# Perceiver block, cross-attention: maxima from row tiles in four visits per group, units in pairs, one stacked key buffer

## The chip, the cores and the metric

One NeuronCore of a Trainium2 chip runs the whole program. The metric is device time in microseconds, the median of several executions; lower is better. The engines are PE (matmuls), DVE (VectorE), ACT (ScalarE), POOL (GpSimd) and SP (SyncE, which here issues DMAs).

## The reference

A block of three layers on x (8 batches of 128 rows, 512 wide). Only the first layer is changed:

```python
x = x + xattn(layernorm(x), ctx_1024, Wq, Wk, Wv, Wo)      # the layer of this change
x = x + attn(layernorm(x), ...)                            # quantised self-attention
x = x + ffn(layernorm(x), router_w, w1, w2)                # eight experts, top two

# xattn: T_q = 128, T_c = 2048, 16 heads of 32
Q = (query @ Wq.T).reshape(B, T_q, 16, 32)
K = (context @ Wk.T).reshape(B, T_c, 16, 32)
V = (context @ Wv.T).reshape(B, T_c, 16, 32)
attn = softmax(einsum('bqhd,bkhd->bhqk', Q, K) / sqrt(32))
out = einsum('bhqk,bkhd->bqhd', attn, V).reshape(B, T_q, 512) @ Wo.T
```

## The kernel before

Cross-attention works batch by batch (b = 0 to 7), and in a batch by groups of four heads (g = 0 to 3). The batches 1 to 6 are a hardware loop on every engine (`Fori(1, B - 1)`); batches 0 and 7 are written out. Operands of a product are split into float16 high and low parts, and a product is three terms (`mm_terms`).

**Projections.** K of a group is made in four blocks of 512 columns (`project_k`), V of eight heads in eight pieces of 2 x 256 columns (`project_v`). All go through two PSUM banks, proj0 and proj1, in the order of the list `USES`; one use of a bank is 12 matmuls of 512 columns or 24 of 256. ACT empties a bank (`copy_v`, or `split_k`, which writes k_hi), DVE makes k_lo, and `wait_bank` lets PE write it again. Some V pieces are cut into thirds and laid between score units (`FILL`, `fill_after`).

**Stacked keys.** For the scores, k_hi, k_lo, k_hi of a head are stacked on 96 partitions of ks, by 12 DMAs that SP issues (`stack_k`, L265); ks has two buffers, so that a group is stacked while the one before is still read. A 97th row (L299, set to 1) meets the negative maximum in qs.

**A group.** First the maxima: eight units u, each two matmuls of 96 x 512 into one of two two-bank tiles sc (`scores_for_max`, L734), and one DVE maximum over 1024 columns (`maximum`, L537). PE lays one third of the next group's K between two units. Then DVE turns the maxima into a diagonal (L545), PE into a row (L749), ACT writes it to qs (L402). Then, for eight units: transposed scores (`scores_transposed`, L763, eight matmuls), the exponential on ACT (L416), and probabilities times V (`times_v`, L780, f32, four column tiles, recorded as 16 matmuls). PE runs one unit of scores ahead of the values.

**Denominators.** DVE sums five of the eight probability units into acc_v (L556, L559), POOL the other three into acc_g (L333, L338), and PE multiplies both, in halves, by ones (`denominators`, L791: 16 f32 matmuls, 32 records).

**Around it.** SP loads the context of the next batch in eight slots' worth of 0.5 MB through two stage buffers (`load_ctx`, L249); ACT writes the high part (L379), DVE the low part (L511), and DVE also the high part of two of the eight. x is loaded in one DMA, and DVE makes its statistics (L578) before group 0. The projection of the output (L821) of batch b - 1 stands in batch b, before group 0. The weights of self-attention are loaded and quantised by POOL beside this.

The experts' loop (`Fori(1, E_ - 1)`, and SP's `Fori(1, E_)`) is the other hardware loop that the change touches.

Of the kernel before, what the change touches and what calls it, by code (L numbers as in the profile page):

```python
# [64 lines left out]
def cross_attention(nc, x, ctxT, wqT, wkT, wvT, woT, wiT, qoT, weights_q, wmax, wscale, x1, x1_stats, ident, ident16, ones, ones16):  # L65

    with ExitStack() as c:
# [3 lines left out]
        def sem(name):  # L73
            return c.enter_context(nc.semaphore(name))

        stage = sb("stage", [P, 2, 2, 512], f32)
# [8 lines left out]
        ks = sb("ks", [P, 2, GH, S], f16)  # L85
# [9 lines left out]
        mx = sb("mx", [P, GH, 2], f32)  # L95
# [19 lines left out]
        sc = [c.enter_context(nc.psum_tensor(f"sc{i}", [P, 1024], f32)) for i in range(2)]  # L115
# [3 lines left out]
        x_in = sem("x_in")  # L119
# [4 lines left out]
        stage_in = [sem(f"stage_in{i}") for i in range(2)]  # L124
# [17 lines left out]
        ks_in = [sem(f"ks_in{i}") for i in range(2)]  # L142
# [8 lines left out]
        stage_hi_v = sem("stage_hi_v")  # L151
# [16 lines left out]
        W_ORDER = (2, 1, 0)  # L168
        w_stage = [probs[:, 0:2, :], probs[:, 2:4, :], v_sb[:, 1, 0:8, :]]
# [5 lines left out]
        USES = ([("k", 0, i) for i in range(KB)] + [("v", 1, i) for i in (0, 1, 2)]  # L175
                + [("k", 1, i) for i in range(KB)] + [("v", 1, 3)]
                + [("k", 2, i) for i in range(KB)] + [("v", 1, i) for i in (4, 5)]
                + [("k", 3, i) for i in range(KB)] + [("v", 1, i) for i in (6, 7)] + [("v", 0, i) for i in range(8)])

        FILL = {0: [(1, i) for i in (6, 7)], 1: [(1, i) for i in range(8, 12)],  # L180
                2: [(1, i) for i in range(12, 16)], 3: [(0, i) for i in range(10, 16)]}
# [11 lines left out]

        def use_k(b, g, kb):
            return 8 + 32 * b + USES.index(("k", g, kb))

        def use_v(b, half, n):
            at = USES.index(("v", half, n))
            return 8 + 32 * b + at if half else 32 * b + at - 24

        def bank(use_in_body):
            return use_in_body % 2

        DVE_HIGH = (2, 3)

        def high_parts_done(b, s):

            if first_batch(b):
                return stage_hi, s + 1
            if s in DVE_HIGH:  # L210
                return stage_hi_v, 2 * (b - 1) + DVE_HIGH.index(s) + 1
            return stage_hi, 8 + 6 * (b - 1) + (s if s > 3 else s + 2) - 1
# [4 lines left out]
        def fill_after(g, unit, last):  # L217

            pieces = FILL[g] if not (last and g == 3) else []
            thirds = [(half, piece, term) for half, piece in pieces for term in range(3)]  # L220
            if unit < 0:
                return thirds[0:3]
            rest = thirds[3:]
            return rest[unit * len(rest) // UNITS:(unit + 1) * len(rest) // UNITS] if unit < UNITS else []

        def wait_k_stacked(eng, b, g):

            if isinstance(b, int) and b == 0 and g == 0:
                return
            n = 2 * b + (g - 1) // 2 + 1 if g else 2 * b  # L230
            eng.wait_ge(ks_in[(g - 1) % 2], 192 * n)

        with nc.Block() as block:

            @block.sync
            def _(sp):
# [4 lines left out]
                def load_ctx(b, s):  # L241
                    n = 8 * b + s
                    if not isinstance(b, int):
                        sp.compute_val(b * (D * S) * 4)
                    if not (first_batch(b) and s < 2):

                        wait_each(sp, (stage_lo, n - 1))
                    src = ctx_v[bass.ds(b, 1), :, 2 * (s % 2):2 * (s % 2) + 2, 512 * (s // 2):512 * (s // 2) + 512]
                    sp.dma_start(stage[:, s % 2], src.rearrange("a p c s -> (a p) c s")).then_inc(stage_in[s % 2], 16)  # L249
# [7 lines left out]
                def stack_k(b, g):  # L257

                    waits = [(proj_act, use_k(b, g, KB - 1) + 1), (k_low, 16 * b + 4 * g + KB)]
                    if g >= 2 or not first_batch(b):  # L260
                        waits.append((s_ready, 8 * (4 * b + g - 1)))
                    wait_each(sp, *waits)
                    for row, part in ((0, k_hi), (HD, k_lo), (2 * HD, k_hi)):
                        for j in range(GH):
                            sp.dma_start(ks[row:row + HD, g % 2, j, :], part[HD * j:HD * j + HD, :]).then_inc(ks_in[g % 2], 16)  # L265
# [4 lines left out]
                load_w(1)  # L270
                load_ctx(0, 2)
                for s in range(3, 8):
                    load_ctx(0, s)
                sp.dma_start(x1[:, :, :], x.rearrange("b p d -> p b d")).then_inc(x_in, 16)
                load_w(2)
                sp.dma_start(wo[:, :, :], woT.rearrange("(c p) d -> p c d", p=P)).then_inc(wo_in, 16)

                def body(b, last):
                    if not first_batch(b):
                        stack_q(b)  # L280
                    stack_k(b, 0)
                    stack_k(b, 1)
                    if not last:
                        load_ctx(b + 1, 0)
                        load_ctx(b + 1, 1)
                    stack_k(b, 2)
                    stack_k(b, 3)
                    if not last:
                        for s in range(2, 8):
                            load_ctx(b + 1, s)  # L290

                body(0, False)
                with sp.Fori(1, B - 1) as b:
                    body(b, False)
# [3 lines left out]
            def _(gp):  # L298
                gp.memset(ks[QK:P, :, :, :], 1.0).then_inc(rows_set, 1)  # L299
# [23 lines left out]
                def body(b, last):  # L323
                    for g in range(G):
# [4 lines left out]

                        gp.wait_ge(e_ready, e + 4)  # L330
# [5 lines left out]
                        gp.wait_ge(e_ready, e + 7)  # L336
                        gp.wait_ge(sum_g, 8 * b + 2 * g + 1)
# [1738 lines left out]
```

## Time and profile before

| what | us |
|---|---|
| median of 3 executions | 2024.96 (2024.83 to 2025.88) |
| the profiled execution | 2023.88 |
| its span, first to last instruction | 2022.4 |
| PE busy | 1767.7 (87%) |
| DVE busy | 1206.1 (60%) |
| ACT busy | 777.4 (38%) |
| POOL busy | 338.0 (17%) |
| mean granted clock of TensorE | 0.941 of full |

Busy time is the union of the instructions of an engine. A matmul's recorded duration overlaps that of the next, since they are pipelined; the distance between starts is its price. Waits are put down to what released them.

### The profile page before, as it was taken

What the parts mean: (1) busy time and instruction counts of PE and PEld (TensorE: products, weight loads), DVE (VectorE), ACT (ScalarE), POOL (GpSimd) and SP (SyncE); (2) the same over time, 40 slices, a digit from 0 to 9 for tenths busy, and PEclk for the clock granted to TensorE, in tenths of its full rate; (3) what the DMA queues carried; (4) which work ended last, traced back from release to release, by engine and by line L of the source; (5) the groups of instructions that cost most, each with busy time, mean ns of one, the idle gap of its engine ahead of it and who ended that gap; (6) DMA issues with size and microseconds to landing.
All of it is one profiled execution on the core that took longest, in us unless ns stands there. A gap on an engine that the chain in (4) does not pass through costs nothing. (4 is left out here: it accounts for less than half of the span.)

```text
span 2022.4 us, 43611 instructions
## 1 busy us (share of the span) xinstructions
PE 1767.7 (87%) x18170; PEld 1171.1 (58%) x18170; DVE 1206.1 (60%) x1469; ACT 777.4 (38%) x955; POOL 338.0 (17%) x308
## 2 busy tenths in 40 slices
PE   6899999999999999999999999774527999999991
PEld 4547557556556556656656655553314777777771
DVE  4477576467467367367377377485765665566632
ACT  4334244244244244344334333228434444444420
POOL 3122111010010010011011046240140000000003
PEclk9999999999999999999999999785857999999996
DMA  6334323133133133133123234400056544554404
GB/s 218 71 89 121 82 66 95 41 85 95 41 85 95 41 84 95 41 79 99 42 72 97 51 87 118 142 1 2 2 188 233 181 164 158 178 192 171 151 14 138
DMA packets 101310, 202.43 MB, mean 100 GB/s; under 512 B 24876, under 2 KB 24876, under 8 KB 101022
## 3 DMA queue, kind: packets, MB, share of 16 engines
q1 hardware_dynamic: 91438, 170.74, 28.8%
q0 software_dynamic: 9712, 29.23, 4.5%
q8 instruction: 140, 2.29, 0.5%
q14 instruction: 20, 0.16, 0.0%
HBM read 127.57 MB, written 18.91 MB: 72 GB/s over the span
## 5 line engine op out<-in xcount | busy, mean ns | idle before, releaser
L537 DVE TENSOR_REDUCE mx<-sc 128x1 f32<-128x1024 f32 x256 | 303.1, 1215 | 23.4 <-PE sc L734 23.2
L416 ACT ACTIVATE probs<-sc 128x1024 f32<-128x1024 f32 x256 | 258.6, 1023 | 146.1 <-PE sc L763 144.1
L559 DVE TENSOR_TENSOR acc_v<-acc_v,probs 128x1024 f32<-128x1024 f32 x96 | 164.4, 1713 | 155.0 <-ACT probs L416 154.4
L396 ACT ACTIVATE k_hi<-proj 128x512 f16<-128x512 f32 x128 | 76.4, 597 | 445.5 <-PE proj L712 445.5
L333 POOL TENSOR_TENSOR acc_g<-probs 128x1024 f32<-128x1024 f32 x32 | 75.5, 2358 | 840.5 <-ACT probs L416 840.5
L734 PE MATMUL sc<-ks,qs 96*128 96x512 f16 x512 | 156.1, 387 | 36.5 <-DVE mx L537 32.1
L699 PE MATMUL proj<-w_hi,ctx_hi 128*128 128x256 f16 x1024 | 156.4, 275 | 20.1 <-DVE ctx_lo L511 20.1
L780 PE MATMUL po<-probs,v_sb 128*32 128x128 f32 x4096 | 163.3, 280 | 9.6 <-ACT probs L416 7.4
L947 DVE SCALAR_TENSOR_TENSOR w_lo<-stage_w,w_hi 128x2048 f16<-128x2048 f32 x64 | 144.4, 2289 | 43.5 <-ACT w_hi L941 43.3
L763 PE MATMUL sc<-qs,ks 97*128 97x128 f16 x2048 | 158.8, 222 | 0.7 <-ACT qs L402 0.7
L699 PE MATMUL proj<-w_hi,ctx_lo 128*128 128x256 f16 x1024 | 155.6, 275 | 0.0
L699 PE MATMUL proj<-w_lo,ctx_hi 128*128 128x256 f16 x1024 | 155.6, 275 | 0.0
L515 DVE SCALAR_TENSOR_TENSOR k_lo<-proj,k_hi 128x512 f16<-128x512 f32 x128 | 88.0, 689 | 113.1 <-ACT k_hi L396 112.7
L1952 PE MATMUL po<-h_lo,w_hi 128*128 128x321 f16 x512 | 154.1, 301 | 0.0
L1952 PE MATMUL po<-h_hi,w_lo 128*128 128x321 f16 x512 | 154.0, 301 | 0.0
L1952 PE MATMUL po<-h_hi,w_hi 128*128 128x321 f16 x512 | 154.0, 301 | 0.0
L712 PE MATMUL proj<-ctx_hi,w_hi 128*128 128x512 f16 x512 | 135.0, 386 | 16.2 <-issue 16.2
L763 PEld LDWEIGHTS sc<-qs,ks 97*128 97x128 f16 x2048 | 122.0, 99 | 38.4 <-issue 29.5
L1788 ACT ACTIVATE hf<-ph 128x321 f32<-128x321 f32 x128 | 56.2, 440 | 220.6 <-PE ph L1936 204.5
L712 PE MATMUL proj<-ctx_hi,w_lo 128*128 128x512 f16 x512 | 135.0, 387 | 0.0
L712 PE MATMUL proj<-ctx_lo,w_hi 128*128 128x512 f16 x512 | 134.6, 386 | 0.0
L780 PEld LDWEIGHTS po<-probs,v_sb 128*32 128x32 f32 x4096 | 98.0, 110 | 58.8 <-issue 37.1
(274 smaller groups left out, 2781.0 us busy)
## 6 DMA issues: line engine op xcount, KB each, us to landing
stage_w<-in_w SPq DMA_DIRECT2D x64, 1024.0 KB, 6.0
stage<-in_ctxT SPq DMA_DIRECT2D x64, 512.0 KB, 4.5
ks<-k_hi SPq DMA_DIRECT2D x256, 128.0 KB, 2.4
ks<-k_lo SPq DMA_DIRECT2D x128, 128.0 KB, 2.4
wq_f<-in_wiT POOLq DMA_DIRECT2D x24, 256.0 KB, 3.0
xbuf<-zeros SPq DMA_DIRECT2D x20, 256.0 KB
obuf<-o_sb POOLq DMA_DIRECT2D x16, 256.0 KB, 2.6
xg<-xbuf POOLq DMA_DIRECT2D x14, 256.0 KB, 5.6
```

The costliest lines, as they stand in the source:

```text
L396: act.activation(k_hi[:, 512 * kb:512 * kb + 512], proj[bank(USES.index(("k", g, kb)))][:, :], ACT.Copy, scale=1.0 / WSCALE).then_inc(proj ...
L416: act.activation(probs[:, u % 4, :], sc[u % 2][:, :], ACT.Exp, scale=1.0 / sqrt(HD)).then_inc(e_ready, 1)
L515: dve.scalar_tensor_tensor(k_lo[:, 512 * kb:512 * kb + 512], proj[bank(USES.index(("k", g, kb)))][:, :], 1.0 / WSCALE, k_hi[:, 512 * kb:51 ...
L537: dve.reduce_max(mx[:, u // 2, u % 2:u % 2 + 1], sc[u % 2][:, :], AX.X).then_inc(m_read, 1)
L559: dve.tensor_tensor(acc_v[:, :], acc_v[:, :], probs[:, (0, 0, 1, 3)[part], :], ALU.add).then_inc(sum_v, 1)
L699: last = pe.matmul(out, x_part[:, kb, e, at:at + P], w_part[:, 2, e, wv], start=term == 0 and e == 0, stop=term == 2 and e == EC - 1)
L712: last = pe.matmul(proj[bank(at)][:, :], w_part[:, 1, e, P * g:P * g + P], x_part[:, kb, e, :], start=term == 0 and e == 0, stop=term == 2 ...
L734: last = pe.matmul(sc[u % 2][:, 512 * i:512 * i + 512], qs[0:QK, 4 * g + j, :], ks[0:QK, g % 2, j, at:at + 512], start=True, stop=True)
L763: last = pe.matmul(sc[u % 2][:, 512 * i + P * j:512 * i + P * j + P], ks[0:QKM, g % 2, j, P * ck:P * ck + P], qs[0:QKM, 4 * g + j, :], sta ...
L780: last = pe.matmul(po[HD * j:HD * j + HD, 0:T], v_sb[:, g // 2, ck, at:at + HD], probs[:, u % 4, 512 * i + P * j:512 * i + P * j + P], sta ...
L947: dve.scalar_tensor_tensor(w_lo[:, s], stage[:, s % NST], WSCALE, w_hi[:, s], ALU.mult, ALU.subtract).then_inc(stage_lo, 1)
L1952: last = pe.matmul(po[i][:, 0:CAP], w_part[:, s, f, P * i:P * i + P], h_part[:, at, :], start=q == 0 and f == 0 and n == 0, stop=q == FQ - ...
```

## The change

1. **Maxima.** ks is no longer read for the maxima. A visit takes one block of 512 keys and all four heads: four matmuls of 32 rows (`tile_position=(32 j, 0)`), q_hi by k_hi, one head per bank of sc, which is now one four-bank tile. One DVE reduction covers the four banks. A group has four visits, and PE lays a whole use of a proj bank between two.
2. **One ks buffer.** ks has room for one group. `stack_k(b, g)` waits for all transposed scores of the group before, and transposed scores of the group wait for it.
3. **Order of uses.** `USES` has eight uses per group: five in the maximum phase (V, the last K block of this group, V, V, V), three in the score phase (K blocks 0 to 2 of the next group). Blocks and pieces of the next batch's first group are made in group 3.
4. **Pairs.** Transposed scores of two units, then values of the two units before, then two thirds of a use. A leading third stands before the first pair.
5. **Denominators.** DVE sums units 0, 1, 4, 5, 6; POOL 2, 3, 7, then adds acc_v, then folds 1024 columns to 512; PE has four f32 matmuls left.
6. **Loads.** Four stage buffers (`SLOTS`) in place of two; ACT makes all high parts of the context; x in two DMAs, the first for batch 0; statistics of the other batches and their roots in the groups 0 and 1 of batch 0. PE waits for wo before batch 0 in place of after it.
7. **Loops.** All loops touched are made by `nc.Fori(..., hint_back_edge=True)`, in cross-attention and in the experts.

```diff
-        ks = sb("ks", [P, 2, GH, S], f16)
+        ks = sb("ks", [P, GH, S], f16)
-        sc = [c.enter_context(nc.psum_tensor(f"sc{i}", [P, 1024], f32)) for i in range(2)]
+        sc = c.enter_context(nc.psum_tensor("sc", [P, GH, 512], f32))
+        FILL_A = [("v", 0, 4), ("k", 0, 3), ("v", 0, 5), ("v", 0, 6), ("v", 0, 7),
+                  ("v", 1, 0), ("k", 1, 3), ("v", 1, 1), ("v", 1, 2), ("v", 1, 3),
+                  ("v", 1, 4), ("k", 2, 3), ("v", 1, 5), ("v", 1, 6), ("v", 1, 7),
+                  ("v", NEXT_V, 0), ("k", 3, 3), ("v", NEXT_V, 1), ("v", NEXT_V, 2), ("v", NEXT_V, 3)]
+        USES = []
+        for g in range(G):
+            USES += FILL_A[5 * g:5 * g + 5] + [("k", g + 1, kb) for kb in range(KB - 1)]
...
                     waits = [(proj_act, use_k(b, g, KB - 1) + 1), (k_low, 16 * b + 4 * g + KB)]
-                    if g >= 2 or not first_batch(b):
-                        waits.append((s_ready, 8 * (4 * b + g - 1)))
+                    if g or not first_batch(b):
+                        waits.append((s_ready, 8 * (4 * b + g)))
...
-                with sp.Fori(1, B - 1) as b:
+                with nc.Fori(1, B - 1, engines=(mybir.EngineType.SP,), hint_back_edge=True) as b:
...
+                        gp.wait_ge(sum_v, at + 4)
+                        gp.wait_ge(sum_g, at + 2)
+                        gp.tensor_tensor(acc_g[:, :], acc_g[:, :], acc_v[:, :], ALU.add).then_inc(sum_g, 1)
+                        gp.wait_ge(sum_g, at + 3)
+                        gp.tensor_tensor(acc_g[:, 0:512], acc_g[:, 0:512], acc_g[:, 512:1024], ALU.add).then_inc(sum_g, 1)
...
+                def maximum(b, g, kb):
+                    dve.wait_ge(m_ready, 16 * b + 4 * g + kb + 1)
+                    dve.tensor_reduce(mx[:, :, kb], sc[:, :, :], AX.X, ALU.max).then_inc(m_read, 1)
...
+                def body(b, last, steps):
+                    for g in range(G):
+                        maximum(b, g, 0)
+                        maximum(b, g, 1)
+                        if g == 3 and not last:
+                            split_ctx(b + 1, 3)
+                        maximum(b, g, 2)
+                        split_k(b, g, 3)
+                        maximum(b, g, 3)
+                        maxima_to_diag(b, g, steps)
...
+                        for part in range(4):
+                            add_probs(b, g, part)
...
+                            if part and (g < 3 or not last):
+                                nb, ng = (b, g + 1) if g < 3 else (b + 1, 0)
+                                split_k(nb, ng, part - 1)
...
+                    for j in range(GH):
+                        rows = slice(HD * j, HD * j + HD)
+                        last = pe.matmul(sc[:, j, :], q_hi[rows, g, :], k_hi[rows, 512 * kb:512 * kb + 512],
+                                         start=True, stop=True, tile_position=(HD * j, 0))
                     last.then_inc(m_ready, 1)
...
+                        scores_for_max(b, g, 0)
+                        if ahead:
+                            project(b, 8 * g)
+                        scores_for_max(b, g, 1)
+                        project(b, 8 * g + 1)
+                        scores_for_max(b, g, 2)
+                        if ahead:
+                            project(b, 8 * g + 2)
+                        scores_for_max(b, g, 3)
+                        if ahead:
+                            project(b, 8 * g + 3)
+                        if g:
+                            denominators(b, g - 1)
+                        elif not first:
                             denominators(b - 1, 3)
+                        if ahead:
+                            project(b, 8 * g + 4, range(2))
+                        maxima_to_row(b, g)
+                        if ahead:
+                            project(b, 8 * g + 4, range(2, 3))
+                        for pair in range(4):
+                            if ahead and pair == 0:
+                                project(b, 8 * g + 5, range(LEAD))
+                            scores_transposed(b, g, 2 * pair)
+                            scores_transposed(b, g, 2 * pair + 1)
+                            if pair:
+                                times_v(b, g, 2 * pair - 2)
+                                times_v(b, g, 2 * pair - 1)
+                            if g == 0 and pair == 0 and not first:
+                                project_out(b - 1)
+                            for i in range(LEAD + 2 * pair, LEAD + 2 * pair + 2) if ahead else ():
+                                project(b, 8 * g + 5 + i // 3, range(i % 3, i % 3 + 1))
```

## Rows read from the trace of the kernel before

**Rows 1.** Timeline of PE: start us, duration, line, operation, count, idle before
```profile
74.05 0.60 PE L734 MATMUL sc<-ks,qs 96*128 96x512 f16 x2 [4.23 <-DMA ks<-k_hi]
...
227.84 3.60 PE L821 MATMUL misc<-wo_sb,ot 128*128 128x512 f32 x8
...
1007.44 3.60 PE L821 MATMUL misc<-wo_sb,ot 128*128 128x512 f32 x8
...
1286.74 5.42 PE L821 MATMUL misc<-wo_sb,ot 128*128 128x512 f32 x8 [1.41 <-DVE ot L568]
```

**Rows 2.** Timeline of PE inside two batches, around and between score phases
```profile
671.30 1.08 PE L780 MATMUL po<-probs,v_sb 128*32 128x128 f32 x32
...
714.34 0.61 PE L699 MATMUL proj<-w_hi,ctx_hi 128*128 128x256 f16 x4
714.78 0.60 PE L699 MATMUL proj<-w_hi,ctx_lo 128*128 128x256 f16 x4
...
717.54 0.64 PE L780 MATMUL po<-probs,v_sb 128*32 128x128 f32 x16 [0.82 <-ACT probs L416]
718.11 0.62 PE L763 MATMUL sc<-qs,ks 97*128 97x128 f16 x8
718.57 0.60 PE L699 MATMUL proj<-w_hi,ctx_hi 128*128 128x256 f16 x4
719.10 0.64 PE L780 MATMUL po<-probs,v_sb 128*32 128x128 f32 x16
...
733.41 0.64 PE L791 MATMUL po<-acc_v,ones 128*32 128x128 f32 x16
...
734.43 0.61 PE L734 MATMUL sc<-ks,qs 96*128 96x512 f16 x2
...
735.73 0.60 PE L734 MATMUL sc<-ks,qs 96*128 96x512 f16 x2
```

**Rows 3.** Groups by line, whole span: busy us, mean ns of one, idle before
```profile
L537 DVE TENSOR_REDUCE mx<-sc 128x1 f32<-128x1024 f32 x256 | 303.1, 1215 | 23.4 <-PE sc L734 23.2
L416 ACT ACTIVATE probs<-sc 128x1024 f32<-128x1024 f32 x256 | 258.6, 1023 | 146.1 <-PE sc L763 144.1
...
L734 PE MATMUL sc<-ks,qs 96*128 96x512 f16 x512 | 156.1, 387 | 36.5 <-DVE mx L537 32.1 <-DMA ks<-k_hi 4.2
...
L515 DVE SCALAR_TENSOR_TENSOR k_lo<-proj,k_hi 128x512 f16<-128x512 f32 x128 | 88.0, 689 | 113.1 <-ACT k_hi L396 112.7
...
L333 POOL TENSOR_TENSOR acc_g<-probs 128x1024 f32<-128x1024 f32 x32 | 75.5, 2358 | 840.5 <-ACT probs L416 840.5
...
L578 DVE BATCH_NORM_STATS2 st<-x 128x6 f32<-128x512 f32 x8 | 4.8, 679 | 3.1 <-DMA x<-in_x 3.1
```

**Rows 4.** Timeline of PE in self-attention: row tiles of 32 and of 17 rows
```profile
1358.75 0.62 PE L1359 MATMUL pa<-k_int,q_int 32*128 32x128 f16 x16 [3.78 <-ACT q_int L1127]
1359.13 0.66 PE L1345 MATMUL pb<-mask_r,mask_l 17*128 17x512 bf16 x4
```

**Rows 5.** Timeline of PE behind a back edge of cross-attention's loop
```profile
675.42 1.51 PE L712 MATMUL proj<-ctx_hi,w_hi 128*128 128x512 f16 x4 [3.04 <-issue]
676.72 1.91 PE L712 MATMUL proj<-ctx_hi,w_lo 128*128 128x512 f16 x4
```

**Rows 6.** Windows, the experts: PE, PEld, DVE, ACT, POOL busy, clock, DMA share, GB/s
```profile
1550.00:1980.00 430.00, 428.64 (x3153) 308.96 (x3151) 248.71 (x362) 173.48 (x227) 21.99 (x39) 1.00 0.43 150
```

**Rows 7.** SP's issues in the timeline, and the landing of the stacked keys (L265)
```profile
31.30 4.21 SPq L276 DMA_DIRECT2D wo_sb<-in_woT  x1
...
63.40 2.77 SPq L265 DMA_DIRECT2D ks<-k_hi  x4
...
745.02 2.42 SPq L265 DMA_DIRECT2D ks<-k_hi  x4
...
DMA to landing us min/median/max: 2.2/2.4/5.4
```

**Rows 8.** The page's DMA issues: count, KB each, us to landing
```profile
wo_sb<-in_woT SPq DMA_DIRECT2D x1, 1024.0 KB, 16.7
```

More of the change, by code:

```diff
@@ L141, in cross_attention @@
         k_low = sem("k_low")
[L142 removed]
+        ks_in = sem("ks_in")
         m_ready = sem("m_ready")
@@ L192, in stacked_q, with use @@
                     for row, part in ((0, q_hi), (HD, q_hi), (2 * HD, q_lo)) for j in range(GH)]
-        def use_k(b, g, kb):
-            return 8 + 32 * b + USES.index(("k", g, kb))
-        def use_v(b, half, n):
[L198 to L212, printed above, removed]
+        def use(b, at):
+            n = FIRST_USES + 32 * b + at
+            if isinstance(b, int) and b == -1 and at == LAST_V:
+                return 0
+            if isinstance(b, int) and b == B - 1 and at > LAST_V:
+                return n - 1
+            return n
@@ L214, in first_batch, with unit_scores @@
+        def unit_scores(u):
+            return sc[:, 2 * (u % 2):2 * (u % 2) + 2, :].rearrange("p a n -> p (a n)")
         def first_batch(b):
             return isinstance(b, int) and b == 0
[L217 to L224, printed above, removed]
@@ L226, in wait_k_stacked @@
         def wait_k_stacked(eng, b, g):
[L228 to L231, printed above, removed]
+            if not (isinstance(b, int) and b == 0 and g == 0):
+                eng.wait_ge(ks_in, 192 * (4 * b + g))
         with nc.Block() as block:
@@ L671, in wait_bank @@
                 def wait_bank(b, at):
[L673 to L680 removed]
+                    if isinstance(b, int) and b == -1 and at in (LAST_V, LAST_V + 3):
+                        return
@@ L694, in project_v @@
-                    kb, at = piece // 4, P * (piece % 4)
-                    wv = slice(256 * half, 256 * half + 256)
-                    for term in terms:
-                        x_part, w_part = mm_terms(ctx_hi, ctx_lo, w_hi, w_lo)[term]
-                        for e in range(EC):
-                            last = pe.matmul(out, x_part[:, kb, e, at:at + P], w_part[:, 2, e, wv],
-                                             start=term == 0 and e == 0, stop=term == 2 and e == EC - 1)
-                    if c == 1 and 2 in terms:
+                    out = proj[at % 2][:, 256 * c:256 * c + 256]
@@ new lines, in project_v @@
+                    kb, col = piece // 4, P * (piece % 4)
+                    if c == 0 and term == 0:
+                        wait_bank(b, at)
+                        if half == NEXT_V:
+                            pe.wait_ge(stage_lo, 8 * (b + 1) + 2 * kb + 2)
+                    wv = slice(256 * (half % 2), 256 * (half % 2) + 256)
+                    x_part, w_part = mm_terms(ctx_hi, ctx_lo, w_hi, w_lo)[term]
+                    for e in range(EC):
+                        last = pe.matmul(out, x_part[:, kb, e, col:col + P], w_part[:, 2, e, wv],
+                                         start=term == 0 and e == 0, stop=term == 2 and e == EC - 1)
@@ L1886, in _ @@
                 body(0, False)
-                with dve.Fori(1, E_ - 1) as e:
+                with nc.Fori(1, E_ - 1, engines=(mybir.EngineType.DVE,), hint_back_edge=True) as e:
                     body(e, False)
```

509 lines of the change are left out of this document (251 added, 258 removed).

## The prediction, made before the result was known

> **What bounds the kernel now.** I read the timeline of PE first, at its landmarks [rows 1]. The output projection of cross-attention (L821) starts at 227.84 and five batches later at 1007.44, so a batch takes 155.9 us; the first maximum scores start at 74.05 and the last output projection ends at 1292.2, so the change has 1292 of 2022 us to work on. Then the timeline inside a batch [rows 2]: PE rows follow each other without a gap through most of a group, so PE sets the pace of this stage. The same rows give its prices. Four V matmuls of 256 columns take 0.44 us (714.34 to 714.78), so one use of a proj bank, 24 of these or 12 K matmuls of twice the width, takes 2.62. Six matmuls of 512 columns take 1.30 (734.43 to 735.73), 0.217 each. Transposed scores of a unit take 0.46 (718.11 to 718.57). The V matmuls before a values unit take 0.53 in place of 0.44 (718.57 to 719.10), and a single values unit 0.57 (717.54 to 718.11), while two in a row take about 0.92 until the last one drains (671.30): 0.46 each, 0.09 to go in and 0.12 to come out. Denominators take 1.02 (733.41 to 734.43). The groups by line add what is idle [rows 3]: PE waits 32.1 us in all for the maxima (L537), 4.0 per batch; the wait for the first exponential of a batch is 0.82 (717.54). DVE's maximum of 1024 columns takes 1.215, ACT's exponential 1.02, k_lo 0.69, GpSimd's add 2.36. None of them is a rival of PE today in their sums (DVE is busy for 60% of the span), so an edit pays in full only where it shortens PE's own list.
>
> **What PE loses.** Sixteen maximum matmuls of a group are 3.5 us. After, there are four visits of four row-tiled matmuls with 32 rows each, on q_hi and k_hi without the stacked copies. The trace has such tiles in self-attention [rows 4]: sixteen of 128 columns start within 0.38 us, 0.024 each, and four of 512 columns are over in 0.66. So four in a visit run side by side: 0.22, and with the 0.21 of changes into and out of a tile mode less their overlap I take 0.38. That is 1.5 per group, a gain of 2.0 (bounds: 0.22 and 0.87 per visit). Denominators fall from 32 recorded matmuls to 8: 0.76. Units in pairs save four of eight changes around the values: 4 x 0.21 = 0.8. Sum per batch 4 x 3.56 = 14.2. The Trainium skill ("TensorEngine Tiling (Array Packing)", Key Properties) says that a change of tiling mode drains TensorE. The 0.09 and 0.12 agree; by that rule the four new visits put back what the pairs take away, and my 0.38 holds it.
>
> **The loops.** At the back edge of PE's loop there is a gap of 3.04 us put down to issue, and the clock falls for the next matmuls (four of them from 676.72 take 1.71 in place of 0.86) [rows 5]. The loop has six passes, so five such edges; I take 3.0 and 1.0 of clock per batch as removed. In the experts PE is busy for 428.6 of 430 us [rows 6], so the same edit there gives nothing. The Trainium skill ("Runtime: NRT & Kernel Launch", Instruction fetch mechanics) says that a taken branch outside the fetched pages stalls for a fetch; the trace agrees in the first loop and not in the second. With the 4.0 and 0.8 of waits gone, PE alone would need 155.9 - 14.2 - 4.0 - 4.8 = 132.9 per batch.
>
> **What is added, in order of time.** The stacked keys ks lose their second buffer. Until now the stack of a group was sent a whole phase early; now its last part, k block 3, is projected between the visits 1 and 2 of its own group, and transposed scores wait for the landing. Follow it from the start of visit 2. Scores end and DVE starts after 0.55; a maximum over four banks is 2 x 1.07 + 0.12 = 2.25 (from the 1.215); k_lo is queued behind it, 0.65; SP 0.1. SP then issues 12 DMAs, four in 2.42 us (745.02) with a pause of 0.05 behind, 0.62 each, and the median landing is 2.4 after its issue [rows 7]: 11 x 0.62 + 2.4 = 9.2, with the longer sets 9.3. With 0.05 the stack is there 12.9 after visit 2. PE has until then: visit and V use 3.0, again 3.0, denominators with their change 0.36, two thirds of a V use 1.75, the row 0.4, the last third 0.87 and the leading K third 0.87, in all 10.25. PE waits 2.65 in every group. Queued behind that wait are all later matmuls of the group, then ACT's exponentials and both engines that add. In group 3 the low part of a context slot stands between two maxima, 0.5 more.
>
> A second wait: with pairs, DVE makes k_lo of block 0 of the next group only after the sum that waits for exponential 4. From pair 2 on: scores 0.63, exponential 1.02, sum 1.25, k_lo 0.69 and links 0.1 are 3.7 to 4.1; PE comes to that bank after 0.92 + 1.13 + 0.87 = 2.94. I take 0.75 per group (bounds 0 and 1.2). The clock: a gap of 3.04 was followed by half speed for some three us; I expect that after half of the new gaps, 1.7 each, less what hides the second wait: 0.6 per group (bounds 0 and 1.7). GpSimd's two added folds (2.36 and about 1.2) end some 4 us after a group and the denominators come 12 after it: nothing on the path, hidden by four proj uses; uncovered they show only in the last group. DVE's maxima save 0.1 us per group, off the path. The visits must not outrun them: 2.25 + 0.55 + 0.06 = 2.86 against 3.0, so no wait, but only 0.14 to spare.
>
> Steady batch: 132.9 + 4 x (2.65 + 0.75 + 0.6) + 0.5 = 149.4.
>
> **The ends.** At the start seven uses stand before the first visit in place of fifteen, x is split in two loads, four slots let the context run ahead; but PE waits for wo, the last load, before its body. wo was issued by 35.5 (31.30 + 4.21) and landed 16.7 later, near 51 [rows 7, 8]; with the same bytes and fewer waits I put the first visit at 50 (bounds 45 and 58). Batch 0 carries seven statistics of x (0.6 each by the x8 row, 4.8 in all) ahead of the maxima of group 1, and sixteen weight maxima between the sums: 8 more. The last batch: three groups of 35.4, which is 16.25 + 2.65 to the scores, then 15.1 (0.92 of scores, 1.73 of K, three times 0.92 + 1.13 + 1.73, and 1.13 of values), 0.75 and 0.6; one output projection 3.5; group 3 without fill: 18.9 to the scores, eight exponentials 9.3, then GpSimd's chain 2.36 + 2.36 + 1.2 + links = 6.2, denominators, reciprocal and product 1.6, projection 5.4: 41.4. Sum 151. The end: 50 + 8 + 7 x 149.4 + 151 = 1254.8, against 1292.2: 37 us less. The rest of the program keeps its 730 us. The profiled execution took 2023.88, 1.1 under the median, its span 2022.4; taken from the median, 2024.96 - 37 = 1988.
>
> **The rivals.** *The stack is hidden*: landings follow faster or the visits are slower than DVE thinks, and the 2.65 and the clock go: 4 x 3.25 + 0.5 per batch, about 106 in all, 1880. For it: SP's rows are issue times, and PE may be slowed by something else ahead. Against: 12 issues of 0.62 stand in the sets that I read, and nothing sends them earlier. *The stack takes longer, and the change is slower*: the only stack for which PE waited took from 63.40 to 74.05, 10.65 in place of 9.3 [rows 1, 7]. 1.35 x 32 is 43: 2031. It decides from 37 / 32 = 1.2 us more per group. Against: that one ran beside the loads of the start. *Row tiles don't run side by side*, the change not doing what it says: 0.87 per visit, three of them ahead of the stack, 1.5 x 32 = 47: 2035; the tile rows speak against it. *The announced loops help the experts too*, by the fetch rule: five edges of 3, 1973; the window without a gap speaks against it.
>
> **How the numbers follow.** Forecast 0.55 (from no lost clock, 1969, and no second wait, 1945, to a start at 58 and a fall after each gap, about 2023); hidden stack 0.15; longer stack 0.20; serial tiles 0.05; experts' loops 0.05. Within 0.2% (4 us, about what this kernel's times can tell from no change) 0.06, out of the upper forecast and the smaller half of the longer stack. Faster 0.74, slower 0.20. The range 1930 to 2034 reaches into the hidden stack by part and over the longer one.
>
> **What would show it.** Right: PE's first transposed scores wait for the DMA of ks by 2 to 3 us in each group; visits 3.0 us apart with four bank-wide matmuls in under 0.4; a batch near 149; no issue gap at the back edge; a K matmul waiting for k_lo in pair 2; the first visit near 50. Wrong if the wait on ks is absent (time near 1880), if it passes 4 us, if GpSimd's reads stretch DVE's maxima, or if DVE falls behind PE's visits, since a late maximum delays visit and stack alike.

## The result, and the profile of the changed kernel

The changed kernel takes 2085.3 us (median of 4, 2079.67 to 2101.22) against 2024.89: 1.032 times as long [1.0293, 1.0347]. Forecast were 1988 and a range from 1930 to 2034. It is slower by 3.2%, and the loss lies in cross-attention: its last output projection ends at 1356.6, where 1292.2 was before and 1254.8 forecast. The program behind it keeps its time (2085.1 - 1356.6 = 728.5 against 730.2).

The first part of the profile's page, after; for each engine busy us, share of the span and instructions:

```profile
PE 1701.8 (82%) x17402; PEld 1138.9 (55%) x17402; DVE 1186.7 (57%) x1333; ACT 784.5 (38%) x972; POOL 450.3 (22%) x372
```

PE is busy for 66 us less and the span is 63 us longer, so PE is idle for about 129 us more. What it waits for stands in the table of PE's waits (us in total, times, longest):

```profile
PE sc L805 <- DMA ks<-k_hi: 87.3, 32, 7.1
PE sc L772 <- DVE mx L567: 69.5, 18, 8.2
...
PE proj L747 <- DVE k_lo L535: 21.7, 29, 1.2
...
PE po L830 <- POOL acc_g L348: 5.7, 1, 5.7
```

The first and third rows are the two waits of the forecast (2.65 x 32 and 0.75 x 29). The second was forecast as nothing, but for the 8 us that batch 0 was given; for maxima PE waited 32.1 before [rows 3]. The landmarks in PE's timeline that answer to [rows 1] are the output projections of batches 0, 1, 5 and 7:

```profile
251.24 3.65 PE L862 MATMUL misc<-wo_sb,ot 128*128 128x512 f32 x8
...
408.29 3.65 PE L862 MATMUL misc<-wo_sb,ot 128*128 128x512 f32 x8
...
1041.51 5.35 PE L862 MATMUL misc<-wo_sb,ot 128*128 128x512 f32 x8
...
1350.30 6.31 PE L862 MATMUL misc<-wo_sb,ot 128*128 128x512 f32 x8 [1.40 <-DVE ot L598]
```

Over the same five batches as in the prediction, a batch is (1041.51 - 251.24) / 5 = 158.1 long (155.9 before, 149.4 forecast); the shortest takes 157.1. The granted clock of 0 to 1290 was 0.98 before and is 0.95 (the two windows, columns as in [rows 6], before ahead of after):

```profile
0.00:1290.00 1290.00, 1200.09 (x12796) 759.76 (x12797) 775.42 (x802) 490.15 (x617) 233.22 (x168) 0.98 0.31 82
```

```profile
0.00:1290.00 1290.00, 1095.12 (x11563) 703.90 (x11563) 731.94 (x644) 478.97 (x613) 317.00 (x206) 0.95 0.30 80
```

Now the place at which PE waits for a maximum in a steady batch, the step from group 2 to group 3. The first visit of group 3 starts at 652.76, the second at 660.23. First PE's timeline (start, duration, line; in brackets the idle time ahead and what ended it), then DVE's and POOL's:

```profile
637.00 1.07 PE L805 MATMUL sc<-qs,ks 97*128 97x128 f16 x16 [2.13 <-DMA ks<-k_hi]
...
647.04 1.04 PE L747 MATMUL proj<-ctx_hi,w_hi 128*128 128x512 f16 x4 [0.63 <-DVE k_lo L535]
...
660.23 0.61 PE L772 MATMUL sc<-k_hi,q_hi 32*128 32x512 f16 x4 [4.34 <-DVE mx L567]
660.77 1.89 PE L747 MATMUL proj<-ctx_hi,w_hi 128*128 128x512 f16 x4
```

```profile
649.77 1.21 DVE L529 TENSOR_TENSOR ctx_lo<-stage,ctx_hi 128x1024 f16<-128x1024 f32 x1
650.90 3.39 DVE L589 TENSOR_TENSOR acc_v<-acc_v,probs 128x1024 f32<-128x1024 f32 x1
654.21 0.68 DVE L535 SCALAR_TENSOR_TENSOR k_lo<-proj,k_hi 128x512 f16<-128x512 f32 x1
654.81 3.06 DVE L529 TENSOR_TENSOR ctx_lo<-stage,ctx_hi 128x1024 f16<-128x1024 f32 x1
657.80 2.28 DVE L567 TENSOR_REDUCE mx<-sc 128x4 f32<-128x2048 f32 x1
```

```profile
650.66 2.55 POOL L343 TENSOR_TENSOR acc_g<-acc_g,probs 128x1024 f32<-128x1024 f32 x1 [5.84 <-ACT probs L435]
654.45 2.34 POOL L346 TENSOR_TENSOR acc_g<-acc_g,acc_v 128x1024 f32<-128x1024 f32 x1 [1.25 <-DVE acc_v L589]
656.87 2.12 POOL L348 TENSOR_TENSOR acc_g<-acc_g 128x512 f32<-128x512 f32 x1
```

The rows show three things. PE's second visit (660.23) can't start until maximum 0 has emptied the only sc tile. Maximum 0 stands in DVE's list behind the last sum and a ctx_lo. And each of these two, which take 1.21 to 1.22 elsewhere (649.77), lasts 1.08 past the end of the POOL add that it meets: 650.66 + 2.55 + 1.08 = 654.29, where the sum ends (650.90 + 3.39); 654.45 + 2.34 + 1.08 = 657.87, where ctx_lo ends (654.81 + 3.06). The same holds the other way: the fold L348, which takes 1.26 where it is alone, starts at 656.87 and takes 2.12. k_lo between them (one operand in PSUM) keeps 0.68 and the maxima 2.28. The Trainium skill ("SBUF — State Buffer", section "SBUF: two separate sides") states this as a rule: a DVE instruction with two inputs in SBUF and a GpSimd instruction that reads SBUF exclude each other for a whole instruction. The rows agree: what is left of each DVE instruction behind POOL's add is nearly the whole of it.

The timeline also shows what such a wait does to the clock. Behind 4.33 to 4.34 us without work the next K matmuls run at the lower of TensorE's two clock levels (four of them take 1.68, 660.77 to 662.45, in place of 0.87). That is so in group 3 of all six loop batches. Behind the waits of 2.1 for ks in groups 1 and 2 of the same batches they keep 0.87.

### The profile page after: what moved, and what is told of

Read it like the earlier page. It is cut to its first block and busy times, and to the rows that moved or that the text cites. A ratio compares the mean times of both kernels' runs of the same rounds, so it can differ in the third digit from the quotient of the medians.

```text
span 2085.1 us, 42258 instructions
## 1 busy us (share of the span) xinstructions
PE 1701.8 (82%) x17402; PEld 1138.9 (55%) x17402; DVE 1186.7 (57%) x1333; ACT 784.5 (38%) x972; POOL 450.3 (22%) x372
## 5 line engine op out<-in xcount | busy, mean ns | idle before, releaser
L435 ACT ACTIVATE probs<-sc 128x1024 f32<-128x1024 f32 x256 | 248.1, 1021 | 238.1 <-PE sc L805 238.1
L567 DVE TENSOR_REDUCE mx<-sc 128x4 f32<-128x2048 f32 x128 | 293.3, 2291 | 73.5 <-PE sc L772 72.8
L589 DVE TENSOR_TENSOR acc_v<-acc_v,probs 128x1024 f32<-128x1024 f32 x96 | 132.5, 1380 | 163.4 <-ACT probs L435 163.2
L805 PE MATMUL sc<-qs,ks 97*128 97x128 f16 x2048 | 141.5, 224 | 87.5 <-DMA ks<-k_hi 87.3
L586 DVE TENSOR_TENSOR acc_v<-probs 128x1024 f32<-128x1024 f32 x32 | 39.2, 1225 | 251.5 <-ACT probs L435 251.5
L399 ACT ACTIVATE v_sb<-proj 128x512 f32<-128x512 f32 x128 | 76.4, 597 | 271.9 <-PE proj L733 271.9
L747 PE MATMUL proj<-ctx_hi,w_hi 128*128 128x512 f16 x512 | 142.3, 403 | 23.5 <-DVE k_lo L535 21.7
L747 PE MATMUL proj<-ctx_hi,w_lo 128*128 128x512 f16 x512 | 151.5, 424 | 0.0
L747 PE MATMUL proj<-ctx_lo,w_hi 128*128 128x512 f16 x512 | 148.6, 417 | 0.0
L822 PE MATMUL po<-probs,v_sb 128*32 128x128 f32 x4096 | 139.4, 277 | 0.1
L991 ACT ACTIVATE w_hi<-stage_w 128x2048 f16<-128x2048 f32 x64 | 119.5, 1904 | 17.3 <-PEq L1098 16.7
```

The lines of the kernel that those rows point to most:

```text
L399: act.activation(v_sb[:, half, 2 * n:2 * n + 2, :], proj[where % 2][:, :].rearrange("p (c d) -> p c d", c=2), ACT.Copy, scale=1.0 / WSCALE ...
L435: act.activation(probs[:, u % 4, :], unit_scores(u), ACT.Exp, scale=1.0 / sqrt(HD)).then_inc(e_ready, 1)
L567: dve.tensor_reduce(mx[:, :, kb], sc[:, :, :], AX.X, ALU.max).then_inc(m_read, 1)
L589: dve.tensor_tensor(acc_v[:, :], acc_v[:, :], probs[:, (0, 0, 1, 2)[part], :], ALU.add).then_inc(sum_v, 1)
L747: last = pe.matmul(proj[at % 2][:, :], w_part[:, 1, e, P * (g % G):P * (g % G) + P], x_part[:, kb, e, :], start=term == 0 and e == 0, stop ...
L805: last = pe.matmul(sc[:, 2 * (u % 2) + i, P * j:P * j + P], ks[0:QKM, j, P * ck:P * ck + P], qs[0:QKM, 4 * g + j, :], start=True, stop=True)
```

## The experiments

Theories, as they stood. **D**: DVE comes late to maximum 0, held by its list and by POOL's adds (the expectations split it: A is POOL's adds, B is the list's order alone). **S**: the stack's issue by one queue sets the wait on ks. Each kernel was run beside the kernel before; ratios are to it. A difference of a few us between two experiments is better taken from the ratios.

**e1_pe_fold.** The denominators go back to PE (16 matmuls a group), POOL keeps its two sums.

```diff
-                        gp.wait_ge(sum_v, at + 4)
-                        gp.wait_ge(sum_g, at + 2)
-                        gp.tensor_tensor(acc_g[:, :], acc_g[:, :], acc_v[:, :], ALU.add).then_inc(sum_g, 1)
...
-                    for j in range(GH):
-                        last = pe.matmul(po[HD * j:HD * j + HD, T:2 * T], ones[:, 0:HD], acc_g[:, P * j:P * j + P],
+                    parts = [(acc, 512 * i) for acc in (acc_v, acc_g) for i in range(2)]
+                    for n, (acc, at) in enumerate(parts):
```

> The changed kernel with the denominators of before: GpSimd makes two sums per group (its third sum and its fold are gone), PE multiplies both accumulators in halves by ones (16 matmuls in place of 4). Theory A, GpSimd's added sums hold DVE's instructions with two SBUF inputs: the low context part at the end of groups 2 and 3 falls from 3.1 to 3.3 us back to 1.22, PE's waits for the maxima from 69.5 us in all to about 35, denominators cost 0.76 x 32 = 24 more on PE, so about 2075 against 2085. Theory B, DVE is late only by the order of its own list: low context part stays over 3 us, the waits stay at 69, time 2105 to 2110.

2050.32 us, 1.0144 [1.0127, 1.0161], 35 less than the changed kernel with, by the prediction's price, 0.76 x 32 = 24 us more of matmuls (2075 was expected). The wait for the maxima halves, as expected, and the context's low part is back at 1215 ns. PE's waits, and DVE's group of ctx_lo in 300 to 1200 us (busy, mean ns):

```profile
PE sc L800 <- DMA ks<-k_hi: 79.1, 32, 6.5
PE sc L767 <- DVE mx L562: 33.9, 13, 4.6
```

```profile
L524 DVE TENSOR_TENSOR ctx_lo<-stage,ctx_hi 128x1024 f16<-128x1024 f32 x48 | 57.8, 1215 | 1.5 <-ACT ctx_hi L382 1.5
```

The same group in the changed kernel:

```profile
L529 DVE TENSOR_TENSOR ctx_lo<-stage,ctx_hi 128x1024 f16<-128x1024 f32 x48 | 81.2, 1703 | 1.5 <-ACT ctx_hi L388 1.5
```

In the profiled executions cross-attention ends 41 us earlier than in the changed kernel. Of these, 12 lie in batch 0, 14 in the next five batches (155.3 each, against 158.1) and 16 behind them. So more than half of the gain lies at the two ends, where POOL also handles self-attention's weights.

**e2_ctx_late.** POOL keeps its folds; the two ctx_lo that stand right ahead of a maximum 0 go behind it.

```diff
                     for g in range(G):
                         maximum(b, g, 0)
+                        if g == 0 and not first:
+                            split_ctx(b, 7)
+                        if g == 3 and not last:
+                            split_ctx(b + 1, 2)
...
-                                if g == 2 and part:
+                                if g == 2 and part in (1, 2):
```

> The changed kernel with one thing moved on DVE: the low context parts 2 (group 2) and 7 (group 3), which stand ahead of the next group's first maximum, are made behind it. Theory A and B both: PE's waits of 4.3 and 2.9 us per batch before visit 1 go; the moved parts cost some 1.3 and 0.7 us later; 5 us per batch, about 2045. Theory C, the wait for the maxima is slack that the stack of keys would take anyway: the wait on the stack grows by as much, time within 5 us of 2085.

2047.74 us, 1.0131 [1.0114, 1.0148], as expected; the wait for maxima falls from 69.5 to 39.4, its longest ones gone from the steady batches, which take 151.8. Mending either half of D alone, the list's order or POOL's adds, takes more than half of the 60 us away: the long wait needs both.

**e3_stack_split.** Six of the twelve DMAs of a stack are issued by ACT.

```diff
-                        for j in range(GH):
+                        for j in (0, 1):
                             sp.dma_start(ks[row:row + HD, j, :], part[HD * j:HD * j + HD, :]).then_inc(ks_in, 16)
...
+                    for row, part in ((0, k_hi), (HD, k_lo), (2 * HD, k_hi)):
+                        for j in (2, 3):
+                            act.dma_start(ks[row:row + HD, j, :], part[HD * j:HD * j + HD, :]).then_inc(ks_in, 16)
```

> The changed kernel with 6 of the 12 DMAs of each key stack issued by ACT in place of SP, so that issuing takes 3.7 us in place of 7.4. Theory S, the wait on the stack is the time of 12 issues in a row: the 87.3 us of waits for the stacked keys fall under 15, time about 2005 to 2010. Rival: the transfers themselves are what takes long (1.57 MB per stack): the waits fall by under 20 us, time over 2065.

2079.63 us, 1.0295 [1.0242, 1.0348]: the waits on ks fall only to 80.3. S falls; the rival, the transfers themselves (over 2065), holds. The timeline of one stack:

```profile
600.27 1.17 SPq L267 DMA_DIRECT2D ks<-k_hi  x2
600.37 1.34 ACTq L390 DMA_DIRECT2D ks<-k_hi  x2
...
602.76 1.59 SPq L267 DMA_DIRECT2D ks<-k_hi  x2
603.04 1.60 ACTq L390 DMA_DIRECT2D ks<-k_hi  x2
...
609.48 0.73 PE L816 MATMUL sc<-qs,ks 97*128 97x128 f16 x10 [2.06 <-DMA ks<-k_hi]
```

The last issue is over at 604.6, and PE starts at 609.48, 9.2 behind the first issue. With one queue it was 9.3 (627.72 to 637.00), with the last issue over at 635.2. The median time from an issue to its landing rises from 2.3 in the changed kernel to between 4.6 and 4.9. So it is the transfer of 12 x 128 KB that takes the time, about 170 GB/s. In the prediction the 9.3 us were built from issues (11 x 0.62 + 2.4). The amount was right and the mechanism wrong.

**e4_klo_first.** k_lo ahead of the sum in each part of DVE's score phase.

```diff
                         for part in range(4):
+                            if part and (g < 3 or not last):
+                                nb, ng = (b, g + 1) if g < 3 else (b + 1, 0)
+                                split_k(nb, ng, part - 1)
                             add_probs(b, g, part)
...
-                            if part and (g < 3 or not last):
-                                nb, ng = (b, g + 1) if g < 3 else (b + 1, 0)
-                                split_k(nb, ng, part - 1)
```

> The changed kernel with k_lo of the next group's blocks made ahead of the sum of probabilities in the same part, not behind it. PE's 21.7 us of waits for k_lo go, 0.7 per group: about 2063 to 2070 if they are on the path that sets the end; within 4 us of 2085 if the next wait takes them up.

2050.0 us, 1.0122 [1.0099, 1.0145], outside both of the expected ranges. The second wait is gone, and 35 us are more than its 21.7: the waits for maxima fell too (from 69.5 to 56.4), and the clock of 300 to 1200 us rose from 0.96 to 0.97.

**f1_pe_late_klo** is e1, e2 and e4 in one; **f2_late_klo** is e2 and e4 with POOL's folds kept. Edits as above.

> The changed kernel with three edits together: denominators of before on PE, low context parts 2 and 7 behind the next first maximum, k_lo ahead of the sums. Theory A (DVE reaches the maxima late, because of its own list and of GpSimd's sums beside it): PE's waits for maxima fall under 20 us in all, for k_lo under 5, the clock comes back to 0.94, time 1995 to 2015. If the three repair the same wait, no more than one of them did alone: 2045.

> As f1, but GpSimd keeps its third sum and its fold (PE has four denominator matmuls). If only the order of DVE's list mattered, this is 24 us faster than f1 (PE's denominators); if GpSimd's reads beside DVE matter in their own right, it is slower than f1. I expect slower, 2015 to 2030, with low context parts and sums still over 2 us where they meet GpSimd.

f1: 2029.71 us, 1.0029 [1.0014, 1.0045], above the 1995 to 2015 that I expected; the three gains (35, 38 and 35) overlap to 56. Its waits for maxima are no shorter than those of e1 (34.3 and 33.9, where under 20 were expected); 7.1 of them lie in five steady batches (36.1 in the changed kernel), the rest in batches 0, 6 and 7. f2: 2045.27, 1.0107 [1.009, 1.0124], slower than f1 as expected, but above its range too. With the list mended, POOL's folds still cost 2045.27 - 2029.71 = 15.6 although they spare PE 24: some 40 us. PE's waits in f1, then in f2:

```profile
PE sc L804 <- DMA ks<-k_hi: 80.9, 32, 6.4
PE sc L771 <- DVE mx L562: 34.3, 29, 6.3
```

```profile
PE sc L809 <- DMA ks<-k_hi: 87.9, 32, 7.7
PE sc L776 <- DVE mx L567: 44.6, 33, 8.5
...
PE po L834 <- POOL acc_g L348: 5.7, 1, 5.7
```

f1 waits 2.6 for POOL's last sum where f2 waits 5.7, so these rows hold 10.3 + 7.0 + 3.1 = 20.4 of the 40; the rest I put down to the clock (0.97 against 0.96 in 0 to 1240), without a run of its own. Nor is the cost spread evenly. In five steady batches f2 is the faster one (150.8 a batch, 151.8 in f1): with the list mended, the folds there cost less than the 3.0 that they spare. f2 loses in batch 0 (its output projection at 250.3, 238.0 in f1) and in the last two batches.

**f3_two_parts.** The stack in two parts: blocks 0 to 2 are sent as soon as their k_lo is there, three quarters of the bytes, and block 3 alone when it is made, half of it by ACT. Two of the context's loads move behind the first part in group 3.

```diff
-                    waits = [(proj_act, use_k(b, g, KB - 1) + 1), (k_low, 16 * b + 4 * g + KB)]
+                    waits = [(proj_act, use_k(b, g, KB - 2) + 1), (k_low, 16 * b + 4 * g + KB - 1)]
...
-                            sp.dma_start(ks[row:row + HD, j, :], part[HD * j:HD * j + HD, :]).then_inc(ks_in, 16)
+                            sp.dma_start(ks[row:row + HD, j, 0:1536], part[HD * j:HD * j + HD, 0:1536]).then_inc(ks_in, 16)
+
+                def stack_late(b, g):
+
+                    wait_each(sp, (proj_act, use_k(b, g, KB - 1) + 1), (k_low, 16 * b + 4 * g + KB))
+                    for row, part in ((0, k_hi), (HD, k_lo), (2 * HD, k_hi)):
+                        for j in (0, 1):
+                            sp.dma_start(ks[row:row + HD, j, 1536:S], part[HD * j:HD * j + HD, 1536:S]).then_inc(ks_in, 16)
```

> The changed kernel with the key stack sent in two parts: blocks 0 to 2 as soon as the scores of the group before have been read and their low parts exist (12 DMAs of 96 KB, SP), block 3 behind its own low part (12 DMAs of 32 KB, half of them issued by ACT). Splitting the issues alone left the wait (80 us of 87): what takes 9.2 us is moving 1.57 MB. Theory T: with 0.39 MB left on the path PE's waits for the stack fall under 20 us and the time to about 2010. Rival: they only turn into waits for the maxima, time over 2070.

1979.52 us, 0.9778 [0.9761, 0.9794]: 106 us less than the changed kernel by this edit alone, where about 75 were expected, and faster than before. The late part is issued as in e3, by two queues; only its bytes are a quarter, so e3 and f3 together show that the bytes set the wait. PE's waits:

```profile
PE sc L796 <- DVE mx L591: 71.0, 18, 9.1
...
PE proj L771 <- DVE k_lo L559: 26.4, 29, 2.0
...
PE sc L829 <- DMA ks<-k_hi: 4.8, 2, 4.6
```

The waits on ks are gone but for one of 4.6 in the last group, the others as they were: the two losses are independent. Over the same five batches a batch takes 147.0 in place of 158.1, or 11.1 less: 8.8 from four waits of 2.1 to 2.4, the rest from the clock (0.98 in 300 to 1200 us, 0.96 in the changed kernel). The rival "the stack is hidden" had priced this at 106.

**f4_all** is f1 and f3 in one.

> f1 and f3 together. With DVE in time and the stack short, PE has its own list left, 136 us per batch (the 132.9 of the prediction and 3 of denominators): cross-attention ends near 1190, time 1910 to 1935. If something else takes the waits over, more than 1960.

1940.4 us, 0.9585 [0.9569, 0.9601], the fastest here, ahead of both kernels, 5 us above the expected range. The output projections of batches 1 and 2 (L889) start at 369.11 and 511.42, 142.3 apart. In five steady batches PE is busy for 135.9 of 142.2 us at a granted clock of 1.00, the 136 that the expectation gave to its list. Left are 34.0 us of waits for maxima and 11.7 on ks (4.5 the longest).

**e5_before_hints** is the kernel before with announced loops; **e6_no_hints** the changed one without.

```diff
-                with pe.Fori(1, B - 1) as b:
+                with nc.Fori(1, B - 1, engines=(mybir.EngineType.PE,), hint_back_edge=True) as b:
```

> The kernel before with the announced loops and nothing else. Theory L: the gap of 3.0 to 3.6 us at PE's back edge in cross-attention goes in all five places, with what it costs of the clock: 16 to 22 us less, 2002 to 2008; the experts keep their 55.40 us each. Rival: the experts gain too, 16 more, about 1988. Rival: the gap is hidden by something else that waits there, within 4 us of 2024.

> The changed kernel with plain loops. If the announcement does the same here as in theory L, the gap comes back five times, 15 to 22 us more than the changed kernel, 2100 to 2107; DVE and SP stand at the same edge, so if their fetches matter too it is over 2115.

e5: 2002.0 us, 0.988 [0.9852, 0.9907], 22.6 less; 20 were forecast, 5 x 4.0. e6: 2098.0, 1.0363 [1.034, 1.0385], 13 more than the changed kernel (9 by the ratios) where 15 to 22 were expected, with five gaps put down to issue, 17.4 us in all. The waits for maxima fall from 69.5 to 57.0 beside them: the gap stands where PE would have waited for a maximum in five of the batches, so 12.5 of it were already lost. In e5 the experts' period stays at 55.4 us, what it is before (1620.40 to 1675.81 to 1731.21): the announced loops give nothing there.

**g1_weights_last** (a single execution). POOL quantises all sixteen weight pieces of batch 7 behind its last group's sums instead of beside groups 0 to 2.

```diff
-                            for n in range(*((0, 6), (6, 11), (11, WPIECES), (WPIECES, WPIECES))[g]):
+                            for n in range(*((0, 0), (0, 0), (0, 0), (0, WPIECES))[g]):
```

> The changed kernel with all sixteen weight pieces quantised by GpSimd behind the last group, not in the groups of batch 7 (one look for the waits; the time itself must be some 40 us longer, since self-attention waits for the pieces). If the weights' transfers and GpSimd's work are what slows the key stack in batch 7, its waits fall from 3.9, 5.7, 6.7 and 7.1 us to the 2.1 to 2.4 of the other batches; otherwise they stay.

PE's first transposed scores of three groups of batch 7, in the changed kernel and then in g1:

```profile
1247.90 1.89 PE L805 MATMUL sc<-qs,ks 97*128 97x128 f16 x16 [5.69 <-DMA ks<-k_hi]
...
1290.20 1.89 PE L805 MATMUL sc<-qs,ks 97*128 97x128 f16 x16 [6.70 <-DMA ks<-k_hi]
...
1330.25 1.89 PE L805 MATMUL sc<-qs,ks 97*128 97x128 f16 x16 [7.12 <-DMA ks<-k_hi]
```

```profile
1242.83 1.07 PE L805 MATMUL sc<-qs,ks 97*128 97x128 f16 x16 [2.10 <-DMA ks<-k_hi]
1277.93 1.07 PE L805 MATMUL sc<-qs,ks 97*128 97x128 f16 x16 [2.06 <-DMA ks<-k_hi]
1315.59 1.89 PE L805 MATMUL sc<-qs,ks 97*128 97x128 f16 x16 [5.48 <-DMA ks<-k_hi]
```

Groups 1 and 2 fall back to the 2.1 of the steady batches, so the weights beside them made their stacks late. Group 3 keeps 5.48, but not because its stack is late: its scores start 12.8 us behind visit 2, as in groups 1 to 3 of a steady batch (12.7). PE comes sooner, since the last group has no V uses to lay between its visits. In the changed kernel it is 14.8 there, 16.3 in group 1 and 17.3 in group 2. Whether the weights' loads or POOL's instructions make the stack late was not told apart. The program as a whole took 2116.38, since the weights now stand ahead of the next stage.

**b1_before_fold** is the kernel before with POOL's two folds and four denominator matmuls, and nothing else of the change.

```diff
+                        gp.wait_ge(sum_v, at + 4)
+                        gp.wait_ge(sum_g, at + 2)
+                        gp.tensor_tensor(acc_g[:, :], acc_g[:, :], acc_v[:, :], ALU.add).then_inc(sum_g, 1)
...
-                    parts = [(acc, 512 * i) for acc in (acc_v, acc_g) for i in range(2)]
-                    for n, (acc, at) in enumerate(parts):
```

> The kernel before with one part of the change alone: GpSimd adds acc_v to acc_g and folds it to 512 columns, PE has four denominator matmuls in place of 16. PE's list is 0.76 us shorter per group, 24 in all. Theory A, what GpSimd reads beside DVE costs DVE as much: DVE's sums and maxima start later, PE waits for maxima more than the 32.1 us of before, time 2015 to 2035. Rival: the fold is free as the prediction had it, 2000. The denominators stand after the fourth unit of the next group's maxima here, some 6 us behind its start, so they may wait for the fold.

2045.75 us, 1.01 [1.0074, 1.0127]: 19 slower where the forecast's terms say 24 faster, and above the 2015 to 2035 expected. PE waits 43.8 for the maxima (32.1 before [rows 3]), 13.0 on ks (4.2), 7.5 for the fold; DVE's ctx_lo has a mean of 1322 ns in place of 1220. So the folds cost about 43 in this kernel too, with another order and other tiles. The three waits hold 28 of them, and the clock of 0 to 1290 is 0.97 in place of 0.98. Here the 7.5 are PE's own wait for the folded sum, so this run also has a cost that the prediction did look for.

## Why the prediction was wrong, step by step

**The step that failed** is "GpSimd's two added folds ... nothing on the path, hidden by four proj uses", with the one that leans on it, "2.86 against 3.0, so no wait". The prediction also took out the 4.0 a batch for which PE waited for maxima before, and put no wait for them in their place; measured are 7.2 in a steady batch. The first step looked at who reads the folded sum, PE's denominators, and they do come late enough in the steady batches. It did not ask what the adds do to DVE meanwhile. DVE's sums and ctx_lo are of the kind that can't run beside them, and at the end of groups 2 and 3 they stand ahead of maximum 0. The second step added up a visit in the steady state. That holds (in groups 1 and 2 the visits start 3.03 to 3.05 apart), but not for maximum 0, which follows DVE's list of the score phase. Of its signs of being wrong, the last came true (a late maximum delays the visit); the one on GpSimd did not, since the maxima were never stretched (2291 ns by mean), the instructions ahead of them were. Price: 69.5 us of waits (4.33 at group 3 and 2.7 to 2.9 at the next group 0, 43 in the six loop batches), and clock. Shown by e1, e2, f2 and b1: the folds cost 59 us in the changed kernel (35 in e1 and the estimated 24 of matmuls), 40 with the list mended (f2 against f1), 43 in the kernel before.

The stretching could be seen in the trace of the kernel before. The page's group of DVE's sums has a mean of 1713 ns:

```profile
L559 DVE TENSOR_TENSOR acc_v<-acc_v,probs 128x1024 f32<-128x1024 f32 x96 | 164.4, 1713 | 155.0 <-ACT probs L416 154.4
```

The first sum of a group, L556, has 1225, and the prediction took 1.25 for all. One L559 starts at 665.74 and takes 1.47, beside a POOL add from 663.77 of 2.36: it too ends 1.08 past the add.

**Right, with their measured sizes.** The visit: four row-tiled matmuls start 0.33 ahead of the next use (0.38 forecast), so they run side by side. The stack: the scores of groups 1 to 3 start 12.7 behind visit 2 (12.9 forecast). The stack's wait: 87.3 us in 32, against 2.65 x 32 + 0.5 x 7 = 88.3; but in the steady batches 2.1 to 2.4 (8.8 a batch, 11.1 forecast), in batch 7 23.4 in all (10.6 forecast), so the close total is luck, and so is the 9.3 of the transfer, which was built from issues (e3). The second wait: 21.7 in 29 (0.75 x 29 = 21.8). The loops: five edges, 22.6 in e5 against 20. The first visit: 48.8 against 50. PE's own list: f4 has 135.9 a batch at full clock, or 132.9 without the 3.0 of its denominators, as forecast. The issue gap at the back edge is gone.

**Mis-sized terms.** *Clock*: I took 0.6 per group, 2.4 a batch. In the five steady batches PE is busy for 139.3 a batch where its list is 132.9 at full clock, so the clock costs 6.4. The forecast had it fall after half of the new gaps; it falls after each 4.33 us wait for a maximum, which was not in the forecast, and again after the 2.1 us wait on ks that follows it in group 3. *Batch 0*: from its score row at 63.56 to that of batch 1 at 245.76 are 182.2; forecast 149.4 + 8 = 157.4. PE waits there for maxima four times, 4.61, 3.73, 4.78 and 8.24. The first is the statistics of x, which the prediction had (4.8). The last is in part the folds again, through a queue that I did not follow. POOL's and DVE's timelines:

```profile
222.11 2.35 POOL L346 TENSOR_TENSOR acc_g<-acc_g,acc_v 128x1024 f32<-128x1024 f32 x1
224.54 2.12 POOL L348 TENSOR_TENSOR acc_g<-acc_g 128x512 f32<-128x512 f32 x1
226.61 0.55 POOL L311 DMA_DIRECT2D wq_f<-in_qoT  x1
```

```profile
229.41 0.69 DVE L681 TENSOR_REDUCE wq_max<-wq_f 128x1 f32<-128x512 f32 x1 [3.87 <-DMA wq_f<-in_qoT]
...
230.63 2.29 DVE L567 TENSOR_REDUCE mx<-sc 128x4 f32<-128x2048 f32 x1
```

POOL issues the load of a weight only behind its two adds, DVE's weight maximum waits 3.87 for it, and maximum 0 and PE are queued behind. In e1, without the folds, the weight maximum waits 1.50 and PE 3.84 in place of 8.24; no run changed the place of the load alone. *Last batch*: 158.7 from its row to the end, against 137. Its stack waits are 23.4 where 2.65 x 4 = 10.6 were counted; g1 ties the excess in groups 1 and 2 to the weights. In group 3 the time from the first visit to the scores is 22.4, and 20.2 in g1, where 18.9 were forecast.

**The sum.** Cross-attention ended 101.8 later than forecast: 24.8 in batch 0, 55.7 in batches 1 to 6, 21.8 in the last, and the start was 0.5 early. A steady batch is 8.7 longer than forecast: 7.2 for the maxima, 4.0 of clock, less 2.3 on ks and 0.4 on k_lo. Over all batches the waits for maxima give 61.5 (69.5 less the 8 that batch 0 was given), and those on ks, 87.3 against 88.3, nothing. That leaves roughly 41. The clock of batches 1 to 6 is about 24 of it, by the 4.0 a batch; the remaining 17 lie in batches 0 and 7, where the clock was lower still (0.92 in 0 to 251, 0.84 in 1205 to 1350), and were not taken apart.

**The rivals.** "The stack takes longer" came true in batch 7 alone and was not what made it slower; f3 shows that the whole stack wait is worth 106 us, just the price of "the stack is hidden"; that the two agree so well is in part luck, since f3 also removes the long waits of batch 7. No run gave the maxima a second sc tile, which might let PE's second visit go ahead of maximum 0. Serial tiles and a help to the experts did not come.

## What to carry to other kernels

When work is moved to an idle engine, look not only for who reads its result but for which instructions of the other engine can't run beside it, and what stands behind those in that engine's list. With one buffer in place of two, send the parts that are ready and leave the last one small: here that took the wait away. The gain of removing an idle stretch can be larger than the stretch (106 us for 82 of waits in f3), and gains of several such edits don't add up (35, 38 and 35 gave 56).

## What was not expected of the hardware

- A DVE instruction with two inputs in SBUF, 1.21 us alone, took 3.06 and 3.39 beside POOL adds of 2.34 and 2.55; it ended 1.08 after POOL's. With one operand in PSUM it kept 0.68.
- Twelve transfers of 128 KB within SBUF took 9.2 to 9.3 us from first issue to use, from one queue or two.
- PE's K matmuls ran at the lower clock level behind each 4.3 us wait of the loop batches, and kept full speed behind the 2.1 us waits of groups 1 and 2.
- Announced loops took 22.6 us off five back edges in the kernel before, and nothing off the experts' loop.
